# Attention products on 32-row groups, weighted values at other places, routing in three parts, and products of zeros in every quad

## The reference

```python
q = split_heads(layernorm(x) @ Wq + bq); k = split_heads(ctx @ Wk + bk); v = split_heads(ctx @ Wv + bv)
scores = einsum('bhqd,bhkd->bhqk', q, k) / sqrt(8)
scores = where(mask == 0, -1e9, scores)
x = x + (softmax(scores) @ v).merge_heads() @ Wo + bo
# then, on layernorm(x):
logits = (h @ w_red) @ wg_normalised.T          # 8 experts
idx = argmax(softmax(logits)); score = max(softmax(logits))
o = gelu(h @ W1[idx] + b1[idx]) @ W2[idx] + b2[idx]
x = x + o * score
```

## Time and profile before

| | |
|---|---|
| device time, median of 3 runs | 248.37 us (247.41 to 249.01) |
| the profiled execution | 249.16 us |
| its span, first to last instruction | 247.3 us |
| mean granted TensorE clock | 0.952 |
| PE / DVE / ACT / POOL busy in the span | 78% / 70% / 55% / 48% |

### The profile page before, as it was taken

The page is one execution under the profiler, slowest core; times in us unless marked ns, Lnnn a source line. Parts: engine busy times, 40 slices in busy tenths (PEclk is TensorE's granted clock), DMA queues, the critical chain, the costliest instruction groups (busy, mean ns, idle before and its releaser), DMA issues.

```text
span 247.3 us, 4771 instructions
## 1 busy us (share of the span) xinstructions
PE 192.6 (78%) x1750; PEld 134.4 (54%) x1750; DVE 173.2 (70%) x454; ACT 135.4 (55%) x271; POOL 119.1 (48%) x231
## 2 busy tenths in 40 slices
PE   0479865998328479776989988988897895999994
PEld 0358653897203177552433543543555784798883
DVE  4678888994684979869767786886755655739252
ACT  2246744939476578435767567667794256260100
POOL 8131768996649857831587784784221022000000
PEclk9999999999955789998899999999999997999999
DMA  5895040000000000000000000000000000000000
GB/s 169 324 398 219 0 170 4 0 4 0 3 1 0 0 0 3 3 3 3 0 0 5 1 0 3 0 3 0 3 1 3 0 0 4 0 3 21 24 21 21
DMA packets 4461, 8.75 MB, mean 35 GB/s; under 512 B 514, under 2 KB 3026, under 8 KB 4052
## 3 DMA queue, kind: packets, MB, share of 16 engines
q1 hardware_dynamic: 3636, 7.78, 8.4%
q10 hardware_dynamic: 800, 0.63, 0.8%
HBM read 7.89 MB, written 0.52 MB: 34 GB/s over the span
## 4 chain that ended last, share of the span: by engine, by line
PE 31%; POOL 29%; DVE 19%; issue 9%; ACT 7%; DMA 2%; SPq 1%; POOLq 0%; DVEq 0%
PE ps L1252 28%; POOL gate_pt L514 6%; POOL rstd L380 5%; POOL w L400 3%; PE ps L1261 3%; POOL x_in L431 3%; DMA wf<-weights_dram 2%; POOL w L392 2%; POOL vareps L377 2%; DVE gate_pt L1033 2%; DVE mx L1090 2%; DVE amax L1027 2%; DVE stats L798 2%; DVE half_c L1080 2%; ACT gate_pt L758 1%
## 5 line engine op out<-in xcount | busy, mean ns | idle before, releaser
L1090 DVE TENSOR_REDUCE mx<-ps 128x2 f32<-128x512 f32 x64 | 42.2, 686 | 16.6 <-PE ps L1252 16.5
L758 ACT ACTIVATE gate_pt<-ps 128x512 f32<-128x512 f32 x64 | 37.2, 603 | 15.6 <-PE ps L1252 15.3
L1252 PE MATMUL ps<-w,hid_xm 128*128 128x256 f16 (+1 forms) x288 | 30.3, 263 | 0.1
L514 POOL TENSOR_SCALAR gate_pt<-ka_mem 32x256 f16<-32x256 f16 x64 | 25.5, 399 | 4.4
L1252 PE MATMUL ps<-gate_pt,half_c 128*128 128x512 f16 x64 | 25.0, 393 | 3.2 <-issue 1.9
L1252 PEld LDWEIGHTS ps<-w,hid_xm 128*128 128x128 f16 x288 | 25.4, 101 | 3.4 <-issue 0.4
L1252 PE MATMUL ps<-qb,gate_pt 128*128 128x256 f16 x128 | 25.4, 281 | 0.8
L1261 PE MATMUL ps<-cst,rows 128*128 128x128 f32 x32 | 7.5, 333 | 18.0 <-ACT rows L662 8.8
L1252 PE MATMUL ps<-gate_pt,hid_xm 128*32 128x256 f32 x256 | 20.4, 390 | 1.5 <-ACT gate_pt L758 1.5
L1252 PEld LDWEIGHTS ps<-qb,gate_pt 128*128 128x128 f16 x128 | 9.5, 99 | 18.7 <-issue 11.4
L380 POOL TENSOR_TENSOR rstd<-vareps,halfs 128x2 f32<-128x2 f32 x24 | 17.7, 738 | 2.0
(11 more groups left out here) (221 smaller groups left out, 505.6 us busy)
## 6 DMA issues: line engine op xcount, KB each, us to landing
stage<-weights_dram SPq DMA_DIRECT2D x2, 1024.0 KB, 11.1
wf<-weights_dram SPq DMA_DIRECT2D x4, 256.0 KB, 8.5
wf<-mask_dram SPq DMA_DIRECT2D x1, 1024.0 KB, 4.8
eb_oT<-ffw_dram SPq DMA_DIRECT2D x1, 768.0 KB, 8.2
ctx_in<-ctx_rows_dram ACTq DMA_DIRECT2D x4, 128.0 KB, 5.9
x_in<-x_dram SPq DMA_DIRECT2D x4, 128.0 KB, 3.1
gate_pt<-ctx_cols_dram SPq DMA_DIRECT2D x1, 512.0 KB, 8.5
out_dram<-ctx_in SPq DMA_DIRECT2D x4, 128.0 KB, 1.7
```

The costliest lines, as they stand in the source:

```text
L514: ins = nc.gpsimd.tensor_scalar(kz[part, n % KRING, k], ka[part, b, quad], 1.0, 0.0, ALU.mult, ALU.add)
L758: nc_act(pt[:, head % PRING].rearrange("p t n -> p (t n)"), ps[:, 2 + head % 2, :], ACT.Exp, scale=DK ** -0.5).then_inc(sig["probs"], 1)
L1090: V.tensor_reduce(mx[:, b, head:head + 2, t], score_bank(4 * n + i).rearrange("p (h n) -> p h n", h=2), AX.X, ALU.max).then_inc(sig["smax" ...
L1252: return nc.tensor.matmul(dst, lhsT, rhs, start=start, stop=stop, skip_group_check=True)
```

## The change

There are five parts.

1. The ring `kz` goes, with POOL's copies (64) and the clearing of the ring. PE's score products read the 32 rows of one head directly: `qa[head rows]` and `ka[head rows]`, `ka` and `qb[head rows]`. Each product has 32 rows, 128 columns and streams 256 columns. Plain scores become two products for each head instead of one of 512 columns for two heads; 64 products of 512 columns become 128 of 256, the 128 shifted ones stay 128.
2. In slot k the shifted scores of head k and the plain scores of head (2, 3, 0, 1)[k] are issued in turn, tile by tile, after both waits: neighbouring products lie on different row groups and write different banks.
3. The weighted values go from slots 0 and 1 to slots 0 and 2.
4. Products of zeros (128x128 by 256 columns, `zeros16` by `ones16`) are added to the banks of the weighted values: two in slot 1 of each quad from 1 on, three in slot 3 of each odd quad, 54 in all.
5. Routing on DVE is cut into three parts at places 12, 13 and 14 of the tail; the router's logits move from place 13 to 12.

```diff
-            def separated_keys(n):
-                b, quad = divmod(n, QUADS)
-                pool.wait_ge(sig["ka_ready"], B + b + 1)
-                if n >= KRING:
-                    pool.wait_ge(sig["st_mm"], 4 * (n - KRING + 1))
-                for k in range(4):
-                    part = slice(32 * k, 32 * k + 32)
-                    ins = nc.gpsimd.tensor_scalar(kz[part, n % KRING, k], ka[part, b, quad], 1.0, 0.0, ALU.mult, ALU.add)
-                ins.then_inc(sig["kz_ready"], 1)
...
-TAIL_STEPS = (0, 2, 4, 6, 10, 13, 15)
+TAIL_STEPS = (0, 2, 4, 6, 10, 12, 15)
+ROUTE_AT = (12, 13, 14)
...
+            def scores_tile(n, i, t, masked):
+
+                b, quad = divmod(n, QUADS)
+                head = rows_of(PLAIN_HEADS[i])
+                dst = score_bank(i)[:, t * T:(t + 1) * T]
+                ins = mm(dst, qa[head, b, quad, t * P:(t + 1) * P], ka[head, b, quad], True, not masked)
...
+            def shifted_tile(n, k, t, masked):
+
+                b, quad = divmod(n, QUADS)
+                tok = slice(t * P, (t + 1) * P)
+                dst = ps[:, 2 + k % 2, t * T:(t + 1) * T]
+                ins = mm(dst, ka[rows_of(k), b, quad, tok], qb[rows_of(k), n % 2], True, not masked)
...
+            def shifted_beside_plain(n, k, masked):
+
+                shifted_wait(n, k)
+                plain = n + 2 < B * QUADS
+                if plain:
+                    scores_wait(n + 2, k)
+                for t in range(TILES):
+                    shifted_tile(n, k, t, masked)
+                    if plain:
+                        scores_tile(n + 2, k, t, masked)
...
+            def zeros_added(n, count):
+
+                m = n // 2
+                for _ in range(count):
+                    mm(ps[:, 4 + m % 2, (n % 2) * T:(n % 2 + 1) * T], zeros16[:, :], ones16[:, 0:T], False, False)
...
                     for k in range(4):
-                        shifted_scores(n, k, masked)
-                        if n + 2 < B * QUADS:
-                            scores(n + 2, k, masked)
+                        shifted_beside_plain(n, k, masked)
                         if k == 1 and n + 1 < B * QUADS:
                             shift(n + 1)
...
-                        if k < TILES and n >= 1:
-                            weighted_values(n - 1, k)
+                        if k % 2 == 0 and n >= 1:
+                            weighted_values(n - 1, k // 2)
+                        if k == 1 and n >= 1:
+                            zeros_added(n - 1, 2)
+                        if k == 3 and n % 2 == 1:
+                            zeros_added(n - 1, 3)
```

More of the change, by code:

```diff
@@ L29 @@
 PRING = 8
-KRING = 4
+PLAIN_HEADS = (2, 3, 0, 1)
 QUADS = NH // 4
@@ L1128, in tail_dve, with route @@
                     lo_part(colsN[:, 1, b], tb[:, 0:T], colsN[:, 0, b], "cols_ready")
-                if step == 5:
+            def route(b, part):
+                if part == 0:
                     dve.wait_ge(sig["logit_mm"], b + 1)
-                    V.tensor_copy(logits[:, b], tb[:, 0:TILES * NE].rearrange("p (t e) -> p t e", t=TILES))\
+                    V.tensor_copy(logits[:, b], tail_bank(b)[:, 0:TILES * NE].rearrange("p (t e) -> p t e", t=TILES))\
                         .then_inc(sig["logits"], 1)
@@ L1137, in tail_dve @@
                     ins.then_inc(sig["top8"], 1)
+                if part == 1:
                     dve.wait_ge(sig["top8"], b + 1)
@@ L1142, in tail_dve @@
                     ins.then_inc(sig["topix"], 1)
+                if part == 2:
                     dve.wait_ge(sig["topix"], b + 1)
@@ L1162, in _ @@
                     now, before = tail_at(n, k), tail_at(*divmod(4 * n + k - 1, 4))
-                    if now and now[1] not in (2, 4):
+                    b, place = tail_place(n, k)
+                    if now and now[1] in (0, 1, 3):
                         tail_dve(*now)
+                    if 0 <= b < B - 1 and place in ROUTE_AT:
+                        route(b, ROUTE_AT.index(place))
                     if before and before[1] in (2, 4):
@@ L1220, in _ @@
             tail_dve(3, 0)
-            tail_dve(2, 5)
+            for part in range(3):
+                route(2, part)
             tail_dve(3, 1)
@@ L1231, in _ @@
             tail_dve(3, 4)
-            tail_dve(3, 5)
+            for part in range(3):
+                route(3, part)
             gelu_lo(1)
@@ L1468, in queries, with rows_of, scores_wait, scores @@
                 ins.then_inc(sig["q_mm"], 1)
-            def scores(n, i, masked):
+            def rows_of(k):
+                return slice(32 * k, 32 * k + 32)
+            def scores_wait(n, i):
                 b, quad = divmod(n, QUADS)
-                t, pair_of = divmod(i, 2)
                 if n == 0 and i == 0:
                     pe.wait_ge(sig["qa_ready"], 1)
-                if i == 0:
-                    pe.wait_ge(sig["kz_ready"], n + 1)
+                if quad == 0 and i == 0:
+                    pe.wait_ge(sig["ka_ready"], B + b + 1)
                 if 4 * n + i >= 2:
                     pe.wait_ge(sig["smax"], 4 * n + i - 1)
-                dst = score_bank(4 * n + i)
-                ins = mm(dst, qa[:, b, quad, t * P:(t + 1) * P],
-                         kz[:, n % KRING, 2 * pair_of:2 * pair_of + 2].rearrange("p h n -> p (h n)"), True, not masked)
-                if masked:
-                    for h in range(2):
-                        ins = mm(dst[:, h * T:(h + 1) * T], idbig[:, :], resmask[:, b, t], False, h == 1)
-                ins.then_inc(sig["s_mm"], 1)
+            def scores_tile(n, i, t, masked):
[3 more added lines that the diff above has]
+                ins = mm(dst, qa[head, b, quad, t * P:(t + 1) * P], ka[head, b, quad], True, not masked)
+                if masked:
+                    ins = mm(dst, idbig[:, :], resmask[:, b, t], False, True)
+                if t == TILES - 1:
+                    ins.then_inc(sig["s_mm"], 1)
+            def scores(n, i, masked):
+                scores_wait(n, i)
+                for t in range(TILES):
+                    scores_tile(n, i, t, masked)
             def shift(n):
```

38 lines of the change are left out of this document (12 added, 26 removed).

## The result

| | before | after |
|---|---|---|
| device time, median (same chip, runs interleaved) | 248.69 us (4 runs) | 258.08 us (4 runs, 257.41 to 259.45) |
| the profiled execution / its span | 249.16 / 247.3 us | 258.15 / 256.1 us |
| mean granted TensorE clock | 0.952 | 0.897 |

The ratio after to before is 1.040, with a 95% interval of 1.035 to 1.045: the change makes the kernel 4% slower, where 2% faster was forecast.

What follows compares the result with a forecast made beforehand. No single bound: PE waits for ACT and DVE in slots 2 and 3, both wait for PE in 0 and 1. Early quads -1.96, tail quads -3.2, rest 0: -5.2 from 249.16, less 0.8, gives 243 us; range 237 to 254.

Steps and rivals of the forecast that it cites:

- the rival: PE's clock stays low from quad 0: 5.42 us a quad, 256 us if half of 13 quads are low; chance 0.20.
- early quads: Five attention quads before the tails: 17.35 us against 19.31, a gain of 1.96 us.
- tail quads: Eight attention quads with tail steps: 34.8 us against 38.02, a gain of 3.2 us.
- The early cycle: A quad goes from 3.69 to 3.47 us; the chain slot 3, exp, weighted values is last and PE idles before it.
- A change of shape: Each switch of PE's array shape costs 0.10 to 0.12 us; 0.7 us added over the eight tail quads.
- Rivals B and D: Score products: row groups don't overlap, 250.4 us; array-shape changes: 0.2 us each, about 248; together chance 0.18.
- base -1.8: Eight tail quads counted at the shorter cycle, 3.47 us each instead of 3.69, before the other tail terms.
- POOL -1.4: Without POOL's key copies, the tail's normed rows reach PE 0.7 us sooner in each of two tails.
- routing in parts: Three smaller routing pieces fit DVE's slack between maxima: 0.4 us gained in each of two tails, 0.8 us.
- zeros: Of 5.8 us of added zeros on PE, those in slot 3 hide under the exp wait; slot 1's are on the path.
- Rival C: Tail steps fall into PE's new idle time; if half is absorbed, 4 us more gain: 239 us; chance 0.12.
- The last two quads: No plain scores there; zeros and shape changes lie under ACT's work: 0 us, with 0 and +1.4 as ends.

Runs made afterwards that it cites:

- c1: The change plus 19 full-size products of zeros ahead of quad 0 and 14 inside it, in both loop branches; 253.43 us, ratio 1.019.
- d1: c1 with its 33 added products of zeros only in the branch that runs; 247.57 us, ratio 0.997 to the kernel before.
- a3: The kernel before plus parts 3, 4 and 5, keeping 128-row score products and POOL's copies; 250.98 us, ratio 1.011.
- b1: The change with each slot's shifted and plain score products on the same row group; 300.24 us, ratio 1.211.
- a4: The kernel before plus 19 full-size products of zeros ahead of quad 0; 248.01 us, ratio 0.999.
- c3: The kernel before with part 3 alone, weighted values in slots 0 and 2; 247.35 us, ratio 0.994.
- c2: The kernel before with part 5 alone, routing in three parts and logits at place 12; 248.76 us, ratio 1.000.
- c4: The kernel before with part 4 alone, the 54 products of zeros; 250.47 us, ratio 1.007.
- d2: d1 with the routing in one piece at its old place 13; 246.19 us, ratio 0.992 to the kernel before.
- d4: The kernel before with c3's spread and 19 full-size products of zeros ahead of quad 0, in the running branch; 247.27 us, ratio 0.997.
- d3: d2 without the change's products of zeros from quad 6 on; 249.45 us, ratio 0.990 to the kernel before.
- b3: The change plus 19 full-size products of zeros ahead of quad 0, every 32-row score product issued twice; 257.81 us, ratio 1.037.
- b4: b2 with its nine extra products per early quad on 32 rows; three executions at 248.4 to 250.9 us, seven at 265.7 to 268.3.
- b2: The change plus 19 full-size products of zeros ahead of quad 0 and nine more in each early quad; 251.77 us, ratio 1.017.

## Why the prediction was wrong, and where it was right

**The step that failed: the clock.** The forecast saw the place (quad 0 falls, 32-row products where it recovered), worked out the right price (5.42 us a quad; measured 5.36 and 5.90), and gave it a chance of 0.20. (The 5.42 was for a quad without zeros in slot 3, so it is the 5.36 that answers to it; at 1.2 GHz those three zeros are not hidden.) What spoke against the rival in the text was that weighted values and zeros keep some full-size work in every quad, and that the clock held through a wait of over a microsecond before. Both are reasons for the clock to stay up, and for that they were not bad: c1 stayed at 1.00 for 58 us on this work (d1, on the same work, only for 40, from copy 0 at 114.34 to 154.1). But the change entered the early quads with the clock down, and what was needed was work that brings it back. There they fail: every low quad but quad 0 has both kinds of work, and the clock stayed low for about six. The run a3 against the change shows that the form of the score products (with the order and POOL's copies that go with it) separates a return within 3.4 us from one after 30.7. The early quads, put at -1.96 us, came to +8.6 (copy 0 to copy 7), and the +1.09 us behind the attention goes with the second low stretch, 3.4 us longer than before. The Trainium skill, "TensorE: Matmul & The Clock Gate", section "Part 1: The HAM clock gate (the "warmup" mystery)", says that the clock is set by how busy PE has been recently. By the busy time of a profile that does not fit this case: b1 was 96% busy for 112.6 us at 0.50, and here the measurement decides.

The price of the rival was right. About six quads were low, and 6 x 1.95 = 11.7 us over the forecast of 243 make 255. Laid out by the ticks, the early quads came 10.6 us over the forecast, the tail quads 3.4 (their missing gain) and the end 1.1, less 1.2 ahead of copy 0: 14.0 us between the forecast -5.2 and the measured +8.8. It was the chance, and with it the upper end of the range (254), that was too low.

**The early cycle was right.** Side by side: starts within 0.01 us. A change of shape behind a pair: 0.09 us (0.10 to 0.12 counted), if a product streams 0.11. The chain from slot 3 over exp to the weighted values comes last, with PE idle before it:

```profile
130.59 0.28 PE L1239 MATMUL ps<-qb,ka_mem 32*128 32x256 f16 x1
...
131.67 0.64 PE L1239 MATMUL ps<-gate_pt,hid_xm 128*32 128x256 f32 x8 [0.28 <-ACT gate_pt L739]
```

(c1, PE's timeline.) The exp of that slot runs 131.02 to 131.62, so the products start 0.05 us after its end where 0.14 was counted; that is the difference between 3.41 and 3.47. Five such quads took 139.97 - 122.86 = 17.11 us, forecast 17.35. (One term of the recorded sum is uneven: exp 2, from 1.41 to 1.96, was given 0.55 us where the others have 0.60; nothing that ends last hangs on it.) Rivals B and D are out. Part of the gain was not the change's, however: the 19.31 us of before contained the fall, and a4, without it, took 134.67 - 115.98 = 18.69 us. Nor is the cycle of 3.41 us the work of the short products: c3 reaches it in quad 5 with the old score products and the spread alone. What the packing adds in the early quads is room for the zeros (a3, the same without packing, takes 3.91 and 3.63 us in quads 4 and 5) and the end of the waits for POOL in quads 2 and 3.

**The second step that failed: the tail quads, -3.2 us.** With the clock at 1.00, copies 6 to 14 of c1 take 178.01 - 139.97 = 38.04 us against 38.02 before: nothing. The terms, from copy 7 to 15:

| term | forecast | measured |
|---|---|---|
| products and POOL (base -1.8, POOL -1.4, shapes +0.7) | -2.5 | -2.50 (change against a3) |
| routing in parts | -0.8 | +0.69 (c2) |
| zeros | 0, hidden in slot 3 | +1.38 (c4) |
| spread | within the base | +0.34 (c3) |
| sum, against the whole change | about -3.2 | -0.09, against +0.24 |

The agreement of the first row is of the sum only; its three terms were not measured apart. The zeros of slot 3 were taken as hidden in front of the wait for exp. That tail steps fill this wait in tail quads is the likely reason why they cost there; it was not measured apart. Of POOL's term, PE's wait for `rows` shows its part: it fell from 1.21 to 0.69 us, 0.52 of the 0.7 counted. But at the step before, the output projection, PE now waits longer for DVE's `y_mem`, 1.20 us (above) where the kernel before has

```profile
144.20 0.33 PE L1252 MATMUL ps<-w,y_mem 128*128 128x128 f16 x3 [0.61 <-DVE y_mem L816]
```

These 0.59 us cancel the 0.52: the tail is a chain over DVE, POOL and ACT, and what PE saves ahead of it PE waits for inside it. The routing was counted as relief for DVE's maxima; but moving the logits to place 12 and cutting the piece gains nothing there. Without it, d2 (one piece, place 13) is 1.2 us quicker from copy 7 to 14 (32.29 us against 33.46 in c1 and in the change). The traces show where: with the logits at place 12, PE waits in each tail for the router's input and then for an exp, and d2 has neither wait.

```profile
158.91 0.29 PE L1239 MATMUL ps<-router,n_mem 128*128 128x8 f16 x6 [0.37 <-DVE n_mem L797]
...
160.77 0.64 PE L1239 MATMUL ps<-gate_pt,hid_xm 128*32 128x256 f32 x8 [0.67 <-ACT gate_pt L739]
```

(The change, PE's timeline.) The quad that holds them takes 5.04 us, in d2 4.38. The reason that was expected for d2, step 6 waiting for the one-hot rows, is not it: that wait is 0.58 us in both. Rival C (tails melt) is out: the waits on `y_mem` and `rows` are still there.

**The rest.** POOL is busy 28.9 us less (about 25 forecast). The last two quads and what is behind 187 us were put at 0; they came to +1.1.

## What to carry to other kernels

Before packing small products, look for low-clock stretches of the old kernel in the same place and ask which work ended them; if the change removes that work, price the whole stretch to the next dense full-height work at the low clock and give it at least an even chance. Ask twice: does the new work hold the clock, and does it bring it back? Undo the parts one by one, and try each alone on the old kernel: here one part of two lines (the spread) gave 0.6% alone (0.3% in d4, within its noise), the best version 0.8%, and the zeros and the routing in parts together cost nearly what the packing earned in the tail quads. Filler products paid here where the engine waits anyway (d1), and cost 2.0 us where the quads are already full (c4); but d3 lost the clock without them. Before counting a gain ahead of a chain over other engines, look for the next wait of that chain: it may grow by as much.

## What the runs showed of the hardware

- The granted clock can stay at 1.2 GHz while PE is busy 94% (the change, 30.7 us) or 96% (b1, 112.6 us), when the score products have 32 rows (88 of the 206 products that start in the stretch of the change). With score products of 128 rows the fall in the same place lasted 3.4 us (a3). Full height is no guarantee: the change's second low stretch, 213.7 to 220.5, has 128-row products alone and lasted 6.8 us.
- 32-row work still counts for holding the clock (b3: 1.00 throughout the attention). The same kernel from quad 1 on stayed at 1.00 for 58 us when it began there (c1) and at 0.50 for 30.7 us when it began there (the change): holding and bringing back are not the same. And near the border one kernel goes either way (b4: 248.4 to 250.9 or 265.7 to 268.3 us). What exactly is counted stays open.
- The fall in quad 0 itself differs between kernels that have the same instructions there: the kernel before, c2 and c4 had it at about 115 us, c3 did not, each in the one execution that was profiled. In a4 its absence is worth 1.1 us in the trace and nothing in the median; this stays open.
- 33 products in a branch that never runs cost 5.9 us of median in one kernel (c1 against d1): PE paused 1.60 us with nothing to wait for, and the clock fell. In b2, with 68 of them, the profile shows nothing of the kind. The cause of the pause stays open.
- Two products on different row groups start 0.00 to 0.01 us apart, and the next pair follows 0.12 us later (0.18 us at 1.2 GHz). On the same row group each starts 0.17 to 0.22 us after the last at 1.2 GHz.
